# Position products of a relative-position attention in blocks of 32 queries instead of 64 (float32, one core)

## The reference, cut to what matters

```
hq = (q @ Wq), hk = (k @ Wk), hv = (v @ Wv)          # 16 heads of 64
attn   = einsum('bidn,bjdn->bijn', hq, hk)           # content
idx    = Lq - 1 - arange(Lq)[:, None] + arange(Lk)[None, :]
b_full = einsum('bidn,jdn->bijn', hq, head_r)        # query x 248 positions
attn   = attn + take_along_axis(b_full, idx[None, :, :, None], axis=2)
attn   = attn + (hk . ub) + (head_r . vb)[idx]
attn   = softmax(attn / sqrt(128), over the keys)
out    = layernorm((attn @ hv * sigmoid(q @ head_w)) @ Wo + residual) * g + b
```

## Time and profile before

| | |
|---|---|
| runs, us | 490.02, 491.75, 492.24; median 491.75 |
| profiled execution, us | 489.52, of which the span from the first to the last instruction is 487.7 |
| granted TensorE clock, mean over the span | 0.989 |
| third stage, us from the span's start | about 185 to the end; its position products from 185.7 to 441 |
| busy in 185 to 487: TensorE, VectorE, ScalarE, GpSimd, us of 302 | 280.56, 258.61, 248.99, 133.60 |

### The profile page before, as it was taken

The page is one execution under the profiler, slowest core; times in us unless marked ns, Lnnn a source line. Parts: engine busy times, 40 slices in busy tenths (PEclk is TensorE's granted clock), DMA queues, the critical chain, the costliest instruction groups (busy, mean ns, idle before and its releaser), DMA issues.

```text
span 487.7 us, 13721 instructions
## 1 busy us (share of the span) xinstructions
PE 447.8 (92%) x4583; PEld 333.7 (68%) x4583; DVE 408.5 (84%) x1316; ACT 381.9 (78%) x1467; POOL 256.7 (53%) x354
## 2 busy tenths in 40 slices
PE   3988999999969999899999999999999999999971
PEld 1654565666546778677878787787787787787750
DVE  4799788888758886598979988988988988888984
ACT  1787798898945556589898898888888888888961
POOL 2467888778746650023433544444444544544584
PEclk9999999999999999999999999999999999999996
DMA  8041000000000003878755854854754764767100
GB/s 239 11 136 62 11 9 10 10 6 6 8 2 1 0 2 93 220 198 192 182 134 122 201 128 110 204 131 110 195 132 113 191 141 115 181 145 190 35 7 22
DMA packets 53335, 48.80 MB, mean 100 GB/s; under 512 B 42912, under 2 KB 48288, under 8 KB 53280
## 3 DMA queue, kind: packets, MB, share of 16 engines
q1 hardware_dynamic: 52704, 47.45, 40.2%
q10 hardware_dynamic: 576, 0.65, 0.4%
HBM read 22.92 MB, written 25.17 MB: 99 GB/s over the span
## 4 chain that ended last, share of the span: by engine, by line
PE 68%; DVE 13%; POOL 5%; issue 4%; ACT 3%; DMA 3%; SPq 2%; DVEq 0%; POOLq 0%; ACTq 0%
PE PS L961 57%; PE PS L1126 5%; PE PS L969 5%; POOL rstd L332 3%; ACT prob L410 1%; DMA rel_scratch<-relw 1%; DMA relr<-rel_scratch 1%; ACT fin L567 1%; DMA ctx<-in_ctxT 1%; DVE xf L815 1%; SPq L234 1%; POOL prob L297 1%; DVE uo L878 1%; PE PS L1228 1%; DVE xn L765 0%
## 5 line engine op out<-in xcount | busy, mean ns | idle before, releaser
L343 POOL TENSOR_TENSOR prob<-prob,rsum 128x480 f32<-128x480 f32 x64 | 65.2, 1018 | 119.8 <-DVE rsum L809 45.2
L483 ACT ACTIVATE prob<-prob,nmax 128x120 f32<-128x120 f32 x256 | 98.2, 392 | 1.7 <-DVE nmax L854 0.8
L410 ACT ACTIVATE prob<-PS,nmax 128x120 f32<-128x120 f32 x256 | 88.8, 408 | 3.6 <-DVE nmax L639 3.6
L297 POOL TENSOR_TENSOR prob<-prob,rsum 128x480 f32<-128x480 f32 x64 | 62.4, 989 | 27.2 <-DVE rsum L688 14.0
L410 ACT ACTIVATION_READ_ACCUMULATOR prob<-PS,nmax 128x1 f32 x256 | 65.2, 255 | 0.0
L961 PE MATMUL PS<-rT,qv 64*64 64x184 f32 x1024 | 52.6, 327 | 6.6 <-ACT fin L567 5.9
L483 ACT ACTIVATION_READ_ACCUMULATOR prob<-prob,nmax 128x1 f32 x256 | 50.7, 198 | 0.0
L969 PEld LDWEIGHTS PS<-ident,prob 128*120 128x120 f32 x256 | 28.0, 138 | 30.1 <-issue 12.1
L961 PEld LDWEIGHTS PS<-xnT,wq 128*128 128x128 f32 x288 | 37.4, 193 | 14.0 <-issue 12.3
L961 PE MATMUL PS<-xnT,wq 128*128 128x128 f32 x288 | 43.2, 288 | 2.1 <-DMA ctx<-in_ctxT 1.4
L969 PE MATMUL PS<-ident,prob 128*120 128x128 f32 x256 | 37.6, 281 | 6.9 <-DVE v L648 3.3
(11 more groups left out here) (192 smaller groups left out, 1115.6 us busy)
## 6 DMA issues: line engine op xcount, KB each, us to landing
rel_scratch<-relw SPq DMA_DIRECT2D x64, 368.0 KB, 4.4
relr<-rel_scratch SPq DMA_DIRECT2D x64, 240.0 KB, 5.3
ctx<-in_ctxT SPq DMA_DIRECT2D x32, 60.0 KB, 1.8
out_x<-fin SPq DMA_DIRECT2D x16, 64.0 KB, 1.6
x_all<-in_x SPq DMA_DIRECT2D x1, 704.0 KB, 7.2
wr<-in_wr SPq DMA_DIRECT2D x1, 512.0 KB, 5.4
wq<-in_wq SPq DMA_DIRECT2D x1, 512.0 KB, 3.6
wk<-in_wk SPq DMA_DIRECT2D x1, 512.0 KB, 4.4
```

What stands on the lines that cost most here:

```text
L297: return pool.tensor_tensor(pr, pr, cols(rsum[p], g, HG).unsqueeze(2).to_broadcast([S, HG, SK]), ALU.mult)
L343: return pool.tensor_tensor(pr, pr, cols(rsum[p], g, HG).unsqueeze(2).to_broadcast([S, HG, SK]), ALU.mult)
L410: last = act.activation(cols(prob[p], n, SK), cols(scores, q, SK), ACT.Exp, bias=nmax[p][:, n:n + 1], accum_out=ssum[p][:, n:n + 1])
L483: last = act.activation(cols(pr, n, SK), cols(pr, n, SK), ACT.Exp, bias=bias[:, n:n + 1], accum_out=total[:, n:n + 1])
```

## The change

The block of queries becomes 32 instead of 64, so WIN becomes 152 instead of 184. Everything that is written in terms of BLK and WIN follows: the position products are 16 calls a group on weight tiles of 64 features by 32 queries with 152 columns instead of 8 calls of 64x64 with 184; ScalarE's copies are 304 columns wide instead of 368; a half is stored by four DMAs of 32 partitions and 1216 elements each instead of two of 64 partitions and 1472; the two waits for a stored half count four DMAs of 16 instead of two. The loads back keep their shape, two DMAs of 64 queries, with a shorter row pitch. VectorE's additions do not change.

```
-BLK = 64
+BLK = 32
 WIN = BLK + SK
...
                     store(t, p, 1)
-                    sp.wait_ge(A1["stored0"], 32 * t + 32)
+                    sp.wait_ge(A1["stored0"], 64 * t + 64)
                     shifted(t, p, 0)
...
-                    sp.wait_ge(A1["stored1"], 32 * t + 32)
+                    sp.wait_ge(A1["stored1"], 64 * t + 64)
                     shifted(t, p, 1)
```

## The result

The changed kernel took 484.72 us in the median of 4 runs (482.15 to 485.40), the kernel before, beside it, 492.0 us (490.02 to 492.54). The ratio is 0.985, with a 95% interval of 0.982 to 0.988: 7.3 us faster, where 6.3 had been forecast (485.5 us, range 481.5 to 497). In a second comparison on another occasion the ratio was 0.987 (0.981 to 0.992), 483.06 against 489.38 us.

The account below looks back on a forecast made before the run. TensorE's work plus a 0.65 us hole was taken to set each step. 6.7 us from 64 groups less 0.4 for the first steps gave 6.3 us: 489.5 to 483.2 profiled, median 485.5 us, range 481.5 to 497.

Parts of the forecast that it names:

- What bounds the kernel: Third-stage step: 18.16 us is TensorE's 17.52 us of work plus one hole; savings on ScalarE alone give nothing.
- the hole of 0.65 us: TensorE, before the fourth group of position products: waits for ScalarE's `fin`, itself waiting for the integer product; forecast to stay.
- The price of a group: TensorE position products: four rounds of 152 columns, 0.51 us, plus 0.14 and 0.03, 0.68 against 0.785; 6.7 us over 64 groups.
- the rest: Group time outside the four rounds: first weight load and hand-over to the next product, 0.165 us before, 0.14 forecast.
- The two corrections inside the rest: TensorE group: 0.025 us less for loading 32-column weights, 0.03 us more for four more starts in a round.
- Eight tiles at once: TensorE: all eight 64x32 tiles run together in four rounds; rival of only four at a time, +24 us, 516 us, chance 0.08.
- The pace floor of 27 ns: Rival on TensorE: matmuls start no faster than 27 ns each, group 1.00 us, +14 us, median 506 us; chance 0.16.
- ScalarE: ScalarE's copies: 64 columns fewer save 54 ns each, 0.43 us a step, worth nothing while TensorE sets the step.
- SyncE and the DMAs: Stores and read backs: four issues take 1.12 to 2.24 us, costed at nothing; rival that transfers take the gain, chance 0.15.
- The first steps: Groups of samples 0 and 1, eight of 64: half their saving counted as lost in waits for first transfers, 0.4 us.

Follow-up runs that it names:

- 184-column run: Kernel before with position products as 16 calls a group on 64x32 tiles, still 184 columns, copies and DMAs unchanged; ratio 1.001 (0.998 to 1.004).
- 76-column run: Changed kernel with only 76 of 152 columns computed in each position product of samples 2 to 15; 470.92 us, ratio 0.961 to the kernel before.
- the four kernels with the old transfers: Kernel before, and it with 64x32 tiles at 184 columns (ratio 1.001), integer product before the third group (0.983), or ScalarE's copies cut to 304 columns (0.998).
- the early product: Changed kernel with the integer product of sample s - 6 made before the third group of position products; 477.14 us, ratio 0.972 to the kernel before.

## Why the prediction was right

- **What bounds the kernel.** TensorE's work plus the hole of 0.65 us, held. Taking 0.42 us off its list took 0.42 off the step; taking the hole off took 0.68; taking 0.43 us off ScalarE took nothing.
- **The price of a group.** Four rounds of columns plus a rest, 0.68 us forecast, 0.67 to 0.68 measured. The rounds were forecast at 0.128 us and are 0.13. The two terms were read from different groups, the 0.84 ns a column from the groups of the kernel before and from `vexp`, the rest from `vexp`; the 184-column run confirms the separation, since the time came back to 0.78 us with the columns alone. The two corrections inside the rest held as well: 0.025 us less for the weight load (0.026 in the starts) and 0.03 more for four more starts in a round (0.027).
- **Eight tiles at once.** This was the open point, with 0.24 of the chance against it. The cuts show eight starts a round. The pace floor of 27 ns is gone: the changed kernel starts a matmul every 16 ns in a round, and the 76-column run holds 13 ns for a whole group. The same runs go against the Trainium skill's 25 ns, in "TensorE: Matmul & The Clock Gate", Part 1, where matmuls go to different tiles; whether it holds on a single tile no run here tests.
- **ScalarE.** Forecast 54 ns a copy and no effect; measured 474 to 421, 53 ns, and no effect.
- **SyncE and the DMAs.** Costed at nothing in a steady step, which held; between the 1.12 and 2.24 us I allowed for four issues stand 1.83. That the read backs issue and land sooner I had not seen.
- **The first steps.** This is the term that was mis-sized. I counted half of eight groups as lost in waits for the first transfers, -0.4 us, and did not ask whether those waits would themselves become shorter. In fact 2.3 us were won by the first read of `relr`, since that place is where the way through DRAM does set the time: the wait of 3.78 us was in the profile. The first sixteen groups, for which the forecast had 1.3 us (16 x 0.105 less 0.4), gave 2.6; the rest gave what the columns say. The whole stretch gained 7.6 us where 64 groups at 0.105 are 6.7, about 0.9 beyond the columns and 1.3 beyond the 6.3 forecast. The 0.9 is no firm number: at the first group of the fifth sample the four kernels with the old transfers stand at 47.5 to 49.1 us and the changed kernel, in its two profiles and with the early product, at 45.8 to 46.1, so after the columns' 1.7 an excess of anything from nothing to 1.6 is left, depending on the execution. The intervals of both comparisons (5.8 to 9.1 us, and 4.1 to 9.1) hold the forecast as well. That the total came within 1 us of the forecast is therefore the columns, rightly priced, and a small term whose sign was wrong.

## What to carry to other kernels

Price small products by rounds: columns of one round, times the rounds when every tile of the array is in use, plus one rest for the first weight load and the hand-over. Halving the tile's width and doubling the number of calls was free here, where the tiles fill the array with either width, so the finer blocking was worth exactly the columns that it avoids. Cutting a group in the timeline at two or three moments gives both terms.

A cover that holds in the steady steps need not hold in the first ones. Look for waits there before a term is put at nothing or at a loss.

If the busiest engine's step is its work plus a hole, a microsecond of the hole is worth as much as one of work: here moving four lines took 0.68 us off a step, the whole change 0.42, and the two add up.

## What the runs showed of the hardware that I had not expected

- One store of two blocks of 32 rows, as a transfer with an outer dimension of 2, turned 484 us into 666 us. Its packet count is 14 a store short of that of the plain form, and mostly 2 rows are under way at a time where the plain form has 15 or more. The bytes, 304 KB a store, are those of two plain stores of 152.
- The time for which an issue holds SyncE's queue depends on what stands ahead: two read backs of the same shape took 2.83 us behind two stores of 368 KB, 2.23 behind two of 304, 1.63 behind four of 184, and 1.31 behind four of 152.
- 32 matmuls on eight tiles and 16 on four tiles, with the same columns, hold TensorE for the same 0.78 us. Within a round of eight the starts are 6 to 7 ns apart.
